# Second attention layer: value products in plain fp32 on two column halves, one exponent per slot, softmax sums added on GpSimd

## The chip, the core and the metric

One NeuronCore of a Trainium2 chip runs the whole program in one launch. The metric is the device time in microseconds (us), as the median of several runs. The engines are TensorE (PE; PEld is its weight load), VectorE (DVE), ScalarE (ACT), GpSimd (POOL) and SyncE (SP, which issues most DMAs). They run their own instruction streams and wait for each other on semaphores.

## What is computed

The program is two decoder layers on `x` (8 batch elements of 100 tokens, 256 wide) with a context `ctx` of 1444 keys of 64 numbers per batch element. The first layer is a causal attention with a mixture-of-experts feed-forward. The change touches only the attention of the second layer:

```python
q_big  = rope(einsum(x @ Wq.T, w_kc_q))          # per head, 192 wide
kv_r   = rope(ctx)                               # (1444, 64), shared by all 16 heads
q_r    = einsum(q_big, W_qr);  k_r = einsum(kv_r, W_kr)
attn   = softmax(einsum(q_r, k_r))               # (16 heads, 100, 1444)
ctx_c  = einsum(attn, kv_r)                      # (16 heads, 100, 64)
x      = x + (ctx_c @ w_kc_kv) @ Wo.T
```

It is followed by an 8-bit quantised gated feed-forward (`bit_linear`). Everything is float32 in and out.

## The kernel before, in words

The second layer runs batch element by batch element (`b` = 0 to 7). One batch element is 48 **slots** (`SLOTS = NG * KT`): four head groups of 4 heads x 100 queries (400 columns, `HT`), and for each of them 12 key tiles of 120 or 121 keys (`KT`). Each engine has one hand-written loop over `b` and slot `s`, and everything that is not a score or a value product is hung on a slot number by the constants at the head of the file.

In a slot PE makes the scores of one key tile (`scores`, L1025 to L1035): two fp32r matmuls, the high parts of q and k against both parts (128 rows) and then the low part of q with a row of negated maxima (65 rows). ACT takes the exponent twice from the same PSUM bank (L1421 into `pt`, plain fp32; L1422 into `ph`, fp32r, which is rounded). POOL subtracts the two (L619) so that `pl` holds the rounded rest. Three slots later (`LAG = 3`) PE adds the value product (`values`, L1037 to L1047): three fp32r matmuls, high weights with high and with low values and low weights with high values. The high value tile has a column of ones, so row 64 of the result is the softmax sum. There are three `pt` buffers and four of `ph` and `pl`.

After each group of 12 slots ACT copies the sum row and the context out of PSUM (`keep_context`), PE turns the sums into a column (`turn_sums`, L1057), DVE inverts them (L1668, 100x4), PE spreads the inverse over 64 partitions (`spread_sums`, L1066), and DVE multiplies (`divide`, L1677). This happens four times per batch element.

Beside this, in slots 0 to 12, the queries and keys of batch element `b + 1` are made: `q_big` (L972, L976) on PE, `rope` on DVE, `q_latent` (L990, 12 matmuls of 64 output columns by 100), `keep_q` on ACT, `low_q` on DVE; `turn_keys` (L1002) with `keep_keys` on ACT. `rotate_keys` on POOL makes the keys of `b + 2` (six pieces). In slots 14 to 40 thirteen **maximum tiles** bound the scores of `b + 1` (`max_tile`, L1017: three fp32r matmuls of 482 columns into three banks; `reduce_max`, L1654: three DVE reductions, which free the banks). The output projection (`attention_out`, L1075, slot 8) and the feed-forward of `b - 1` (`turn_xq`, `gate_and_up`, `turn_hq`, `ffn_down` on PE; `quantise_x`, `hidden`, `quantise_h` on DVE; `norm_x4` and `norm_h` on POOL; a Silu and a Square on ACT) are hung on slots 8 to 41. Batch element 7 has no next one to prepare, and batch element 0 has no feed-forward beside it.

On PE all of this is one in-order stream; a wait stops all that stands behind it. On POOL, `norm_x4` and `norm_h` stand in the same queue as the subtractions.

## Time and profile before

| what | us |
|---|---|
| median of 3 runs (1206.18 to 1210.96) | 1210.91 |
| the profiled execution: its own time | 1210.05 |
| its span, first to last instruction | 1208.0 |
| start of batch element 0's slots | 442.7 |
| one batch element in the middle (b = 3, 718.1 to 813.8) | 95.7 |
| slots of the last batch element | 1101.0 to 1172.6 |
| busy: PE, DVE, ACT, POOL | 1050.0, 530.6, 565.0, 579.8 |
| mean granted TensorE clock | 0.914 of 2.4 GHz |

Busy times are of the whole span, which has stages with different limits, so the stages have to be read one by one. A plain fp32 matmul leaves two MATMUL records in the trace, an fp32r matmul one. The length of a matmul's record includes the time for its results to arrive; what a matmul costs in a stream is the distance between two starts.

### The profile page before, as it was taken

The page shows a single profiled execution, that of the slowest core. Times are in us where ns is not written, and L with a number is a line of the kernel's source. Part 1 is how long each engine was busy: PE and PEld are TensorE (multiplying, and loading weights), DVE is VectorE, ACT ScalarE, POOL GpSimd, SP SyncE. Part 2 cuts the span into 40 slices and gives each one's busy share as a digit, 9 for nine tenths or more (in the row PEclk, how much of TensorE's full clock was granted, in tenths as well). Part 3 has the DMA queues.
Part 4 walks back from the last instruction along what each step waited for, and adds up shares of the span by engine and source line. Part 5 has one row for each costly group of instructions (what it writes and reads, how often), then busy time and mean ns, then how long its engine had stood idle before and what let it go on. Part 6 is the DMA issues. An engine that isn't in the chain of part 4 may idle for free.

```text
span 1208.0 us, 18195 instructions
## 1 busy us (share of the span) xinstructions
PE 1050.0 (87%) x6674; PEld 841.2 (70%) x6674; DVE 530.6 (44%) x1063; ACT 565.0 (47%) x1205; POOL 579.8 (48%) x787
## 2 busy tenths in 40 slices
PE   6986776788882879999999999999999999999883
PEld 3665665457872748888788678778778778877572
DVE  3234552333202663544743653563473473472423
ACT  2322222101212215765765664764665675577761
POOL 2002230244004007767676676676677575376760
PEclk9767887889996969999999999999999999999986
DMA  9015001516761000000000000000000000000000
GB/s 242 4 48 162 1 1 50 197 39 220 269 222 46 1 13 1 1 14 1 1 17 1 1 17 2 1 17 1 1 1 17 1 1 5 1 1 5 1 4 3
DMA packets 37827, 49.25 MB, mean 41 GB/s; under 512 B 9798, under 2 KB 31352, under 8 KB 37484
## 3 DMA queue, kind: packets, MB, share of 16 engines
q1 hardware_dynamic: 36716, 46.46, 12.4%
q0 software_dynamic: 1024, 1.64, 0.4%
q8 instruction: 53, 0.87, 0.3%
q14 instruction: 34, 0.28, 0.1%
HBM read 42.73 MB, written 5.31 MB: 40 GB/s over the span
## 4 chain that ended last, share of the span: by engine, by line
PE 61%; DVE 14%; issue 9%; POOL 6%; ACT 6%; DMA 2%; SPq 0%; POOLq 0%; DVEq 0%; ACTq 0%
PE ps L1033 8%; PE ps L990 5%; PE ps L972 5%; DVE nm L1654 5%; PE ps L913 4%; PE ps L1017 4%; PE ps L1047 4%; PE ps L1044 4%; PE ps L1045 4%; POOL pl L619 3%; PE ps L976 3%; PE ps L1075 2%; PE ps L1066 2%; PE ps L926 2%; PE ps L734 2%
## 5 line engine op out<-in xcount | busy, mean ns | idle before, releaser
L619 POOL TENSOR_TENSOR pl<-pt,ph 120x400 fp32r<-120x400 f32 (+1 forms) x384 | 407.5, 1081 | 282.4 <-ACT ph L1422 238.6
L1421 ACT ACTIVATE pt<-ps 120x400 f32<-120x400 f32 (+1 forms) x384 | 193.8, 505 | 154.3 <-PE ps L1033 150.7
L1654 DVE TENSOR_REDUCE nm<-ps 128x1 f32<-128x482 f32 (+1 forms) x312 | 184.1, 650 | 39.7 <-PE ps L1017 39.1
L1422 ACT ACTIVATE ph<-ps 120x400 fp32r<-120x400 f32 (+1 forms) x384 | 192.0, 500 | 0.0
L1033 PE MATMUL ps<-qh,khl 128*120 128x400 f32 (+1 forms) x384 | 149.7, 390 | 8.8 <-ACT ph L1422 5.6
L1033 PE MATMUL ps<-ql,kh 65*120 65x400 f32 (+1 forms) x384 | 135.1, 352 | 0.0
L1047 PE MATMUL ps<-pl,kv 120*65 120x400 f32 (+1 forms) x384 | 134.2, 349 | 0.4 <-POOL pl L619 0.2
L1044 PE MATMUL ps<-ph,kv 120*65 120x400 f32 (+1 forms) x384 | 134.2, 350 | 0.0
L1045 PE MATMUL ps<-ph,kv 120*64 120x400 f32 (+1 forms) x384 | 133.5, 348 | 0.0
L1017 PE MATMUL ps<-khl,qh 128*128 128x482 f32 (+1 forms) x312 | 101.5, 419 | 6.1 <-DVE ql L1646 1.7
L1633 DVE TENSOR_TENSOR xyz<-ps,ropeq 128x400 f32<-128x400 f32 x64 | 33.8, 570 | 157.3 <-PE ps L976 157.3
L1033 PEld LDWEIGHTS ps<-qh,khl 128*120 128x120 f32 (+1 forms) x384 | 72.0, 188 | 31.1 <-ACT ph L1422 9.9
L1354 ACT ACTIVATE qh<-ps 64x400 fp32r<-64x400 f32 x64 | 31.8, 497 | 116.7 <-PE ps L990 116.3
L1017 PEld LDWEIGHTS ps<-khl,qh 128*128 128x128 f32 (+1 forms) x312 | 57.9, 193 | 32.0 <-DVE nm L1654 14.5
L568 POOL TENSOR_TENSOR sm<-sm,mx 100x1600 f32<-100x1600 f32 x8 | 22.9, 2862 | 112.9 <-DVE mx L1501 112.9
L1033 PEld LDWEIGHTS ps<-ql,kh 65*120 65x120 f32 (+1 forms) x384 | 72.4, 189 | 4.2
L990 PE MATMUL ps<-xyz,amat 128*64 128x100 f32 x768 | 72.7, 251 | 0.2 <-DVE ql L1646 0.2
L990 PEld LDWEIGHTS ps<-xyz,amat 128*64 128x64 f32 x768 | 66.5, 137 | 5.5 <-issue 3.4
L972 PE MATMUL ps<-x3T,wqb 128*128 128x100 f32 x512 | 67.3, 288 | 2.8 <-DVE xyz L1637 2.2
L972 PEld LDWEIGHTS ps<-x3T,wqb 128*128 128x128 f32 x512 | 65.7, 204 | 5.1 <-DVE xyz L1637 2.5
L1047 PEld LDWEIGHTS ps<-pl,kv 120*65 120x65 f32 (+1 forms) x384 | 52.7, 137 | 20.5 <-POOL pl L619 2.4
L1045 PEld LDWEIGHTS ps<-ph,kv 120*64 120x64 f32 (+1 forms) x384 | 53.3, 139 | 18.2
(250 smaller groups left out, 1592.8 us busy)
## 6 DMA issues: line engine op xcount, KB each, us to landing
egu<-_L_ffn_gate_up_proj_dram SPq DMA_DIRECT2D x14, 1024.0 KB, 5.6
edn<-in_L_ffn_down_proj_dram SPq DMA_DIRECT2D x14, 512.0 KB, 6.4
craw<-in_ctx_dram SPq DMA_DIRECT2D x8, 360.0 KB
wo_n<-in_L_xattn_Wo_dram SPq DMA_DIRECT2D x1, 2048.0 KB, 11.7
wq_n<-in_L_xattn_Wq_dram SPq DMA_DIRECT2D x1, 2048.0 KB, 9.7
xs_scratch<-zero SPq DMA_DIRECT2D x1, 1792.0 KB, 12.9
xs<-xs_scratch SPq DMA_DIRECT2D x14, 128.0 KB, 5.5
ys_scratch<-ysb SPq DMA_DIRECT2D x14, 128.0 KB, 5.8
```

The lines of the kernel that those rows point to most:

```text
L619: nc.gpsimd.tensor_tensor(pl[k % PS_BUF][r, :], pt[k % PT_BUF][r, :], ph[k % PS_BUF][r, :].bitcast(F32), ALU.subtract).then_inc(pl_ready, 1)
L913: last = mm(ps[:, 2 * (t % 2) + a, TR * m:TR * m + TR], egu[t % EBUF][:, c, FI * a + 128 * m:FI * a + 128 * m + 128], xsT[t % 2][:, c, :], ...
L972: mm(ps[:, 4, S * i:S * i + S], wqb[:, c, h, 0:128], x3T[:, c, :], start=c == 0, stop=c == DC - 1)
L990: last = mm(ps[0:CD, 6, S * i:S * i + S], amat[:, h, j, :], xyz[k % 2][:, j, i, :], start=j == 0, stop=j == 2)
L1017: mm(ps[0:w, max_bank(b, i) + n, 0:MN], qh[b % 2][:, 128 * i:128 * i + w], khl[b % 2][:, MSTART[n]:MSTART[n] + MN], start=True, stop=True) ...
L1033: last = mm(ps[0:key_rows(t), k % 2, 0:HT], lhs[:, keys], rhs[:, HT * c:HT * c + HT], start=first, stop=not first)
L1044: mm(bank[0:CD + 1, :], w[r, t, CD:2 * CD + 1], hi[r, :], start=t == 0, stop=False)
L1045: mm(bank[0:CD, :], w[r, t, 0:CD], hi[r, :], start=False, stop=False)
L1047: mm(bank[0:CD + 1, :], w[r, t, CD:2 * CD + 1], lo[r, :], start=False, stop=t == KT - 1).then_inc(pv_done, 1)
L1421: nc.scalar.activation(pt[k % PT_BUF][0:rows, :], ps[0:rows, k % 2, 0:HT], ACT.Exp)
L1422: nc.scalar.activation(ph[k % PS_BUF][0:rows, :], ps[0:rows, k % 2, 0:HT], ACT.Exp).then_inc(ph_ready, 1)
L1654: nc.vector.tensor_reduce(nm3[0:w, i, n:n + 1], ps[0:w, max_bank(b, i) + n, 0:MN], AX.X, ALU.max)\
```

## The change

- Scores: a slot is still one key tile by one head group, but two slots in a row now take the same key tile for groups c and c + 2. A **pair** of slots is one step of the value product; there are 24 pairs and two rounds of 12 (`LANE` = 24 slots) per batch element.
- ACT takes one exponent per slot, into one half of `pt` (5 buffers of 120 x 2 x 400, plain fp32).
- The value product of a pair is two plain fp32 matmuls of 64 output columns, group c into partitions 0 to 63 and group c + 2 into partitions 64 to 127 of one bank. The value tile is the plain 64 columns.
- The softmax sums: POOL adds the `pt` tiles of a round (`add_weights`, 11 additions of 120x800 per round, each waiting for the one before), PE sums over the partitions with a matrix of ones (`sum_weights`, two matmuls), DVE inverts 128x400 and multiplies 128x400 (`divide`). The turn, the spread and the copy of the sum row are gone.
- `rotate_keys` loses a copy and a subtraction; the low part of the keys is made by DVE from PSUM (`low_keys`, three of 64x480 per batch element).
- `q_latent` writes two heads on the two column halves in turn; `keep_q` and `low_q` become four and two instructions of half the width.
- `max_tile` uses only the high parts, 64 rows each: tiles 0 and 2 on rows 0 to 63, tile 1 on rows 64 to 127. Its first matmul waits for the second reduction of the tile before, not the first.
- Some slots move by one or more; the divide stands at slot 7 of a round.

```diff
-KEEP_AT, TURN_AT, SPREAD_AT = 3, 4, 5
+KEEP_AT, SUM_AT, DIVIDE_AT = 3, 5, 7
-KEY_SLOT = (8, 9, 11)
+KEY_SLOT = (9, 10, 12)
-OUT_SLOT = 8
+OUT_SLOT = 9
-X4_SLOT, H_NORM_SLOT = 10, 24
+X4_SLOT, H_NORM_SLOT = 11, 24
-PT_BUF, PS_BUF = 3, 4
+PT_BUF = 5
@@ rotate_keys (POOL)
-            step(nc.gpsimd.tensor_tensor(kraw[r, :, :], kcos[r, :, :], ksin[r, :, :], ALU.add))
-            step(nc.gpsimd.tensor_copy(k[r, t, CD:2 * CD], kraw[r, :, :]))
-            nc.gpsimd.tensor_tensor(k[r, t, 0:CD], kraw[r, :, :], k[r, t, CD:2 * CD].bitcast(F32), ALU.subtract)\
-                .then_inc(kv_ready, 1)
+            nc.gpsimd.tensor_tensor(k[r, t, :], kcos[r, :, :], ksin[r, :, :], ALU.add).then_inc(kv_ready, 1)
@@ new (POOL), called in every odd slot
+        def add_weights(pool, j):
+            q, t = j // KT, j % KT
+            pool.wait_ge(p_ready, 2 * j + 2)
+            if t == 0:
+                return
+            r, total = slice(0, key_rows(t)), acc[q % 2]
+            if t == 1 and q >= 2:
+                pool.wait_ge(sums_done, q - 1)
+            if t > 1:
+                pool.wait_ge(p_added, (KT - 1) * q + t - 1)
+            before = pt[(j - 1) % PT_BUF] if t == 1 else total
+            nc.gpsimd.tensor_tensor(total[r, :, :], before[r, :, :], pt[j % PT_BUF][r, :, :], ALU.add).then_inc(p_added, 1)
@@ POOL's loop
-                    nc.gpsimd.tensor_tensor(pl[k % PS_BUF][r, :], pt[k % PT_BUF][r, :], ph[k % PS_BUF][r, :].bitcast(F32),
-                                            ALU.subtract).then_inc(pl_ready, 1)
+                    if s % 2:
+                        add_weights(pool, PSLOTS * b + s // 2)
@@ q_latent (PE)
-                for i in range(HG):
-                    h = HG * g + i
+                for i in range(0, HG, 2):
                     for j in range(3):
-                        last = mm(ps[0:CD, 6, S * i:S * i + S], amat[:, h, j, :],
-                                  xyz[k % 2][:, j, i, :], start=j == 0, stop=j == 2)
+                        for a in range(2):
+                            last = mm(ps[CD * a:CD * a + CD, 6, S * (i // 2):S * (i // 2) + S], amat[:, HG * g + i + a, j, :],
+                                      xyz[k % 2][:, j, i + a, :], start=j == 0, stop=j == 2)
@@ max_tile (PE)
-                    if before >= 0:
+                    if before >= 0 and n:
                         pe.wait_ge(m_reduced, 3 * before + n + 1)
-                    mm(ps[0:w, max_bank(b, i) + n, 0:MN], qh[b % 2][:, 128 * i:128 * i + w],
-                              khl[b % 2][:, MSTART[n]:MSTART[n] + MN], start=True, stop=True).then_inc(m_done, 1)
+                    elif before >= 0:
+                        pe.wait_ge(m_reduced, 3 * before + 2)
+                    r, keys = slice(CD * (n % 2), CD * (n % 2) + CD), khl[b % 2] if n % 2 else kh1[b % 2]
+                    mm(ps[0:w, max_bank(b, i) + n, 0:MN], qh[b % 2][r, 128 * i:128 * i + w],
+                              keys[r, MSTART[n]:MSTART[n] + MN], start=True, stop=True).then_inc(m_done, 1)
@@ values and the sums (PE)
-                mm(bank[0:CD + 1, :], w[r, t, CD:2 * CD + 1], hi[r, :], start=t == 0, stop=False)
-                mm(bank[0:CD, :], w[r, t, 0:CD], hi[r, :], start=False, stop=False)
-                pe.wait_ge(pl_ready, k + 1)
-                mm(bank[0:CD + 1, :], w[r, t, CD:2 * CD + 1], lo[r, :], start=False, stop=t == KT - 1).then_inc(pv_done, 1)
+                for a in range(2):
+                    last = mm(ps[CD * a:CD * a + CD, 2 + q % 2, 0:HT], kv[b % KV_BUF][r, t, :], pt[j % PT_BUF][r, a, :],
+                              start=t == 0, stop=t == KT - 1)
+                last.then_inc(pv_done, 1)
+            def sum_weights(q):
+                pe.wait_ge(p_added, (KT - 1) * (q + 1))
+                if q:
+                    pe.wait_ge(c_ready, q)
+                for a in range(2):
+                    last = mm(ps[CD * a:CD * a + CD, 7, 0:HT], ones[0:KP, :], acc[q % 2][:, a, :], start=True, stop=True)
+                last.then_inc(sums_done, 1)
@@ ACT's loop
-                    nc.scalar.activation(pt[k % PT_BUF][0:rows, :], ps[0:rows, k % 2, 0:HT], ACT.Exp)
-                    nc.scalar.activation(ph[k % PS_BUF][0:rows, :], ps[0:rows, k % 2, 0:HT], ACT.Exp).then_inc(ph_ready, 1)
+                    if j >= PT_BUF and k % 2 == 0:
+                        act.wait_ge(pv_done, j - PT_BUF + 1)
+                        act.wait_ge(p_added, added(j - PT_BUF))
+                    nc.scalar.activation(pt[j % PT_BUF][0:rows, k % 2, :], ps[0:rows, k % 2, 0:HT], ACT.Exp).then_inc(p_ready, 1)
@@ divide (DVE)
-                tt(ct[p, cols], ctu[p, cols], ps[p, 7, 0:HT], ALU.mult).then_inc(c_ready, 1)
+                step(nc.vector.reciprocal(inv[:, :], ps[:, 7, 0:HT]))
+                tt(ct[:, cols], ctu[:, cols], inv[:, :], ALU.mult).then_inc(c_ready, 1)
```

## Rows read from the trace of the kernel before

**Rows 1.** The page: span and busy times of the engines.

```profile
span 1208.0 us, 18195 instructions
PE 1050.0 (87%) x6674; PEld 841.2 (70%) x6674; DVE 530.6 (44%) x1063; ACT 565.0 (47%) x1205; POOL 579.8 (48%) x787
```

**Rows 2.** Busy time by stretch (b = 3 in four parts, b = 0, b = 7).

```profile
core 0: us, PE busy (x) PEld busy (x) DVE busy (x) ACT busy (x) POOL busy (x), PEclk, DMA share, GB/s
718.10:757.60 39.50, 39.23 (x305) 34.43 (x303) 13.31 (x33) 19.62 (x43) 27.03 (x50) 1.00 0.02 5
757.60:776.70 19.10, 17.29 (x86) 12.74 (x86) 9.68 (x20) 14.66 (x29) 10.73 (x13) 0.91 0.00 0
776.70:808.10 31.40, 30.64 (x174) 23.50 (x173) 25.39 (x47) 20.42 (x45) 23.72 (x22) 1.00 0.01 2
808.10:813.80 5.70, 5.70 (x35) 4.76 (x33) 0.81 (x2) 4.98 (x12) 4.07 (x5) 1.00 0.21 51
...
442.70:528.00 85.30, 84.10 (x525) 70.61 (x526) 38.00 (x75) 52.49 (x118) 60.61 (x83) 0.95 0.03 10
...
1101.00:1172.60 71.60, 63.97 (x348) 49.92 (x347) 22.96 (x33) 52.23 (x113) 49.93 (x50) 0.93 0.01 2
```

**Rows 3.** Timeline of PE in ordinary slots: start us, length us, engine, line.

```profile
620.39 0.34 PE L1033 MATMUL ps<-qh,khl 128*120 128x400 f32 x1
620.57 0.34 PE L1033 MATMUL ps<-ql,kh 65*120 65x400 f32 x1
...
621.30 0.34 PE L1033 MATMUL ps<-qh,khl 128*120 128x400 f32 x1
```

**Rows 4.** Timeline of PE around a query product and a spread of sums.

```profile
633.50 2.27 PE L990 MATMUL ps<-xyz,amat 128*64 128x100 f32 x24
...
635.70 0.45 PE L1033 MATMUL ps<-qh,khl 128*120 128x400 f32 x1
635.99 0.34 PE L1033 MATMUL ps<-ql,kh 65*120 65x400 f32 x1
...
636.53 0.34 PE L1047 MATMUL ps<-pl,kv 121*65 121x400 f32 x1
636.81 0.90 PE L1066 MATMUL ps<-ident,inv 100*64 100x100 f32 x8
637.64 0.45 PE L1033 MATMUL ps<-qh,khl 128*120 128x400 f32 x1
637.92 0.34 PE L1033 MATMUL ps<-ql,kh 65*120 65x400 f32 x1
```

**Rows 5.** Timeline of PE in the set-up: two fp32 products on column halves.

```profile
79.98 0.65 PE L739 MATMUL ps<-woT,kckv_n 128*64 128x256 f32 x4
80.56 0.66 PE L722 MATMUL ps<-ident,wo_n 128*128 128x128 f32 x4
```

**Rows 6.** Groups of POOL instructions by shape: busy us, mean ns.

```profile
L619 POOL TENSOR_TENSOR pl<-pt,ph 120x400 fp32r<-120x400 f32 x256 | 270.6, 1073 | 189.1 <-ACT ph L1422 148.0 <-issue 28.2 <-PE ps L1047 7.4
L568 POOL TENSOR_TENSOR sm<-sm,mx 100x1600 f32<-100x1600 f32 x8 | 22.9, 2862 | 112.9 <-DVE mx L1501 112.9
L503 POOL TENSOR_TENSOR kraw<-kcos,ksin 120x128 f32<-120x128 f32 x32 | 14.6, 457 | 2.5
```

**Rows 7.** Groups of DVE reciprocals by shape.

```profile
L1668 DVE RECIPROCAL inv<-ps 100x4 f32<-100x4 f32 x32 | 5.7, 180 | 49.4 <-PE ps L1057 49.3
L1530 DVE RECIPROCAL rec<-ps 100x16 f32<-100x16 f32 x8 | 2.0, 252 | 2.9 <-PE ps L844 2.9
```

**Rows 8.** Groups on DVE in 776.7 to 808.1.

```profile
L1654 DVE TENSOR_REDUCE nm<-ps 128x1 f32<-128x482 f32 (+1 forms) x33 | 19.5, 650 | 3.2 <-PE ps L1017 3.1
L1716 DVE SCALAR_TENSOR_TENSOR h<-h,rstdh,lnw_b 100x1024 f32<-100x1024 f32 x1 | 1.3, 1286 | 0.0
L1677 DVE TENSOR_TENSOR ct<-ctu,ps 64x400 f32<-64x400 f32 x2 | 1.1, 563 | 0.2 <-PE ps L1066 0.2
```

**Rows 9.** Timeline of POOL and DVE in the last batch element.

```profile
1118.97 7.09 POOL L619 TENSOR_TENSOR pl<-pt,ph 120x400 fp32r<-120x400 f32 x7
1119.04 5.15 DVE L1692 TENSOR_SCALAR xn<-x_sb,mv,rstd 100x256 f32<-100x256 f32 x1 [2.77 <-POOL rstd L529]
...
1142.71 6.03 DVE L1716 SCALAR_TENSOR_TENSOR h<-h,rstdh,lnw_b 100x1024 f32<-100x1024 f32 x1 [3.41 <-POOL rstdh L529]
```

**Rows 10.** The chain that ended last: the last division.

```profile
1177.77 0.58 DVE ct L1677
```

168 lines of the change are left out of this document (72 added, 96 removed).

## The prediction

> **What bounds the kernel now.** I read the page first [rows 1]: PE is busy 87% of the span, no other engine over half. Then the busy times by stretch [rows 2], because the second layer (442.7 to the end) is where the change lies. In the middle of the layer one batch element takes 95.7 us, and I cut it in four by what runs beside the slots. Slots 0 to 12 (39.5 us, with the queries and keys of the next element) have PE busy 39.2: PE sets the pace. Slots 13 to 22 (19.1 us) have 1.8 us of PE idle and wait on the feed-forward's chain through DVE, POOL and ACT. Slots 23 to 41 (31.4 us) have PE busy 30.6 and DVE 25.4, which is close behind. Slots 42 to 47 (5.7 us) are PE alone. The last element takes 71.6 us with PE idle for 7.6. Then the timeline for what a matmul costs: an ordinary slot is five fp32r matmuls from 620.39 to 621.30, so 0.91 us, or 0.182 each [rows 3].
>
> **What the change does to PE in a slot.** Removed: three value matmuls, 3 x 0.182 = 0.546 us per slot. Added: per pair two plain fp32 matmuls of 400 columns on the two column halves. The trace has the same thing in the set-up: L739 is two fp32 products of 256 columns on two column halves, four records, in 0.65 us, and the next group starts 0.58 us after it [rows 5]. A record of 256 columns at fp32 is 256 x 2 / 2.4 GHz = 0.213 us, so four in a row would start the next group after 0.85; two and two are 0.43, and 0.58 is that and 0.15 for the ends. So the halves run side by side. For 400 columns: 2 x 0.333 = 0.667 us per pair.
>
> **The ends are the catch.** Between an fp32r matmul of full width and a product of 64 columns the stream stops [rows 4]. L1047 starts at 636.53 and has 0.167 of columns, so it is through at 636.70; L1066 starts at 636.81: 0.11 us lost, and about 0.05 until its first weights are in. L1066's eight records start 0.083 to 0.086 apart and are through at 637.54; the next score matmul starts at 637.64, and the one behind it 0.28 later instead of 0.182, because its weights were not loaded ahead: 0.19 us lost. After L990 it is the same (635.70 to 635.99). I take 0.35 us for going there and back, so a value pair costs 0.667 + 0.35 = 1.02 us against 2 x 0.546 = 1.09 now. The plain slots gain almost nothing. (The Trainium skill, "TensorEngine Tiling (Array Packing)", Key Properties, states that changing the tiling mode drains the engine; this rule speaks against the change, the rows above agree with it, and without it the pair would be 0.67.)
>
> **Other PE terms, per batch element.**
> - The turn and the spread of sums go, four times. From L1047's end (636.70) to the next score matmul's real start (637.74) the spread is 1.0; the turn I take as the same. 4 x 2.0 = 8 us.
> - `sum_weights`, two times: one more value pair, 1.0 each, 2 us. It waits for POOL's last addition of the round; the cover is five slots of PE work (over 4 us, over 7 where `q_big` lies between), and POOL needs about 2 per addition, so it costs nothing unless POOL is more than two additions behind.
> - `q_latent`: 24 records 0.086 apart (2.27 with the end) [rows 4] become 12 pairs: 1.03 saved, four times, 4.1 us. It had the switch already.
> - `turn_keys` has 64 output columns now and gets the switch, 3 x 0.3 = 0.9 us.
> - `max_tile`: three matmuls of 482 columns are 3 x 0.2 = 0.60. With two of them side by side they are 0.40, and the switch adds 0.35: +0.15, thirteen times, +1.9 us. Bounds: 0.2 less each if there is no switch, +0.35 if the row halves don't overlap.
>
> **Stage by stage, b = 1 to 6.** Slots 0 to 12: -13 x 0.546 - 2.0 - 4.1 = -13.2; +6.5 x 1.02 + 1.0 + 0.9 = +8.5; so PE -4.7. `q_big` of the second group waits for DVE's rope of the first, which now has some 2 us of slots before it instead of 3.9 and needs about 2.7: +0.7. Stage: -4.0.
> Slots 13 to 41: PE -29 x 0.546 - 2 x 2.0 = -19.8; +14.5 x 1.02 + 1.0 + 1.9 = +17.7: -2.1. But here DVE is the next limit. It is busy 35.1 of the 50.5 us [rows 2], and the rest of its time is mostly waits in the feed-forward chain that stay. It loses two inversions and two multiplications of 0.56 and 0.18 [rows 7, 8], -1.5, and gains one `divide`: the reciprocal of 128x400. The rows give 180 ns at 4 elements and 252 at 16, so 6 ns each: 0.16 + 400 x 0.006 = 2.5 us, the upper bound; one like a multiplication of 400 (0.56) is the lower; I take 2.5, the only rows of the same operation. With the multiplication 3.1. So DVE gains 1.6 us. Further it is held by POOL (below), +2 to +4. I take -1.0 for the stage.
> Slots 42 to 47: PE -0.2; zero. Sum per element: -5. Six of them: -30.
> Element 0 has no feed-forward, so PE's sums hold: -4.7 - 2.1 - 0.2 = -7.
>
> **POOL.** An addition of 120x800 is in no row. 457 ns at 128 elements and 1073 at 400 [rows 6] are 2.26 ns an element, so 1.98 us; by the 100x1600 row (2862) it is 1.67. I take 2.0 and 0.08 for the wait on the one before. 22 per element are 46 us, the rotated keys 6 x 1.6 = 10, the norms 1: 57 of some 90 us. POOL is behind a pair in the plain slots (2.08 against PE's 4 x 0.182 + 1.02 = 1.75) and catches up elsewhere; five buffers carry that. ACT has half its exponents and is nowhere the limit; `low_keys` and the halves of `low_q` and `keep_q` add some 2.5 us to DVE in slots 0 to 12, where it is busy 13.3 of 39.5 [rows 2]; that cover would have to shrink by half before it shows.
>
> **The last element.** From 1101.0 to the last division, 1177.77 [rows 10], it is 77.4 us. POOL sets the pace now: 22 x 2.08 + norms + 3 us start + some 3 us of waits for the norms = 53, then the sum, the reciprocal and the multiplication (4.5), and stalls of the feed-forward that the buffers don't cover, 5: 63. That is -14; I give it 0 to -20, as PE's clock is less sure there (0.93 now). The start-up of element 0 (DVE-bound maxima) I leave at 0 to +2.
>
> **Sum:** -30 - 7 - 14 = -51, and +1 for the start, -50. Against the profiled execution's own time, 1210.05 (0.9 below the median of the three runs), 1160 us.
>
> **The rivals.**
> 1. *No drain, or a cheaper one.* If the weights for the value pair are pulled ahead of the scores, 0.35 x 24 = 8.4 us of PE per element go. In slots 0 to 12 and for element 0 they are time, in slots 13 to 41 DVE keeps most of it: about -4 per element and -8 for element 0, so -35: 1125. Against it: three transitions of the same two kinds in the rows, all with it. For it: DVE or POOL may set the pace so that the drains lie in waits.
> 2. *DVE held by POOL* (slower). In the last element DVE's L1692 takes 5.15 us while POOL runs seven subtractions back to back, and L1716 takes 6.03 where it takes 1.29 undisturbed [rows 8, 9]. POOL's additions are twice as long, and six DVE instructions per element read and write only SBUF in this way (three in `quantise_x`, three in `quantise_h`), and the new multiplication of `divide`. I have counted 2 to 4 us per element, because each addition waits for the one before and leaves a gap. If two of them per element are held for 5 to 6 us instead, that is +9 in slots 13 to 41, PE waits behind `turn_xq` and the maxima, and the sum turns: 1160 + 7 x 9 = 1223. It decides from 7 us per element. (The Trainium skill, "SBUF — State Buffer", describes the pair of ports that DVE and GpSimd share as an exclusive lock held for a whole instruction. By it each holding is one addition, up to 2 us, seven times 1 on average: the sum above plus about 3 per element, 1180; the 5.15 us row shows more than one instruction.)
> 3. *The halves don't overlap* (slower). Then a value pair is 1.33 + 0.35, 16 us more per element, and `q_latent` and the sums 5.5: 1160 + 8 x 21 = 1330. Rows 5 speak against it.
> 4. *The clock.* Slots 13 to 22 have a mean of 0.91 [rows 2], so 19.1 x 0.09 x 2 = 3.4 us of them at 1.2 GHz. If PE, with more short gaps, gets one more such stretch per element, each costs 1.7: 1174. It is within my range.
>
> **How the numbers follow.** Forecast (1140 to 1185, with rival 4) 0.60; rival 1 and cheaper terms (1095 to 1140) 0.21; between 1185 and 1204 0.05; no change 0.04; rival 2 0.08; rival 3 0.02. A measurement of this kernel tells 0.5%, 6 us, from no change. The likeliest value is 1160; eight in ten lie in 1105 to 1205. Faster by over 0.5%: 0.86, within: 0.04, slower: 0.10.
>
> **What would show it.** Right: two MATMUL records of the value pair starting within some 10 ns of each other, twice per pair; value pair and switch near 1.0 us between score matmuls; an element near 90 us; a reciprocal of 2.5 us; additions near 2.0; DVE busy over 37 us in slots 13 to 41. Wrong: score matmuls behind the values with their weights loaded ahead, an element under 85; DVE instructions of several us beside the additions; PE idle in slots 42 to 47 for POOL; a granted clock below 0.9 in the middle of the layer.

## The result and the profile after

The changed kernel takes 1285.97 us (median of 4 runs, 1282.71 to 1288.57) beside 1210.93 for the kernel before on the same chip (1206.18 to 1216.58): the ratio is 1.0616, with a 95% interval of 1.0564 to 1.0669. It is 6% slower; the forecast was 4% faster.

The page of the changed kernel, its span and busy times. Against [rows 1] there is less work of every kind but DVE's, and PE is busy for 18 us *longer*:

```profile
span 1281.0 us, 15373 instructions
PE 1068.0 (83%) x5842; PEld 655.6 (51%) x5842; DVE 598.5 (47%) x1087; ACT 397.6 (31%) x837; POOL 473.6 (37%) x480
```

832 fewer matmuls and more busy time are longer matmuls. A part of it is by design, since each of the two records of a plain fp32 matmul is longer than that of an fp32r one; the rest shows in the granted clock. Of both kernels the busy times from the first slot to the last of the layer: span, busy of PE, PEld, DVE, ACT and POOL, then the granted clock, DMA share and GB/s. First the kernel before:

```profile
442.70:1172.60 729.90, 703.25 (x4424) 572.43 (x4425) 355.78 (x719) 462.59 (x991) 490.92 (x612) 0.98 0.02 5
```

and the changed kernel:

```profile
444.50:1242.10 797.60, 727.49 (x3604) 391.32 (x3604) 416.96 (x736) 293.94 (x615) 390.45 (x333) 0.81 0.02 5
```

The granted clock of the whole layer falls from 0.98 to 0.81. The levels are 1.00 (2.4 GHz) and 0.50 (1.2 GHz), nothing between. Added up, the stretches at 0.50 from the layer's first slot to the end of the span are 55.3 us before and 338.1 after.

The same batch element as in [rows 2] (b = 3, slots 0 to 12, 13 to 22, 23 to 41, 42 to 47), then three windows within it and the last element's slots:

```profile
762.50:797.60 35.10, 32.90 (x279) 24.66 (x277) 17.57 (x38) 12.86 (x31) 19.12 (x27) 1.00 0.02 6
797.60:819.50 21.90, 19.21 (x63) 8.06 (x60) 10.98 (x20) 11.39 (x21) 10.36 (x11) 0.69 0.00 0
819.50:861.00 41.50, 36.77 (x130) 15.74 (x129) 28.84 (x45) 11.59 (x23) 18.50 (x11) 0.74 0.00 1
861.00:867.20 6.20, 6.20 (x28) 3.08 (x26) 0.81 (x2) 2.95 (x7) 3.57 (x2) 0.84 0.25 64
802.00:815.00 13.00, 13.00 (x34) 5.30 (x35) 7.94 (x15) 4.14 (x7) 6.55 (x4) 0.50 0.00 0
815.50:839.00 23.50, 19.74 (x83) 8.10 (x82) 19.60 (x29) 10.94 (x20) 11.84 (x7) 1.00 0.00 1
839.10:861.00 21.90, 20.66 (x62) 9.18 (x62) 10.64 (x19) 4.31 (x8) 7.50 (x4) 0.50 0.00 1
...
1181.20:1242.10 60.90, 55.65 (x240) 28.43 (x238) 24.81 (x29) 27.83 (x56) 43.06 (x25) 0.89 0.01 2
```

Slots 0 to 12 take 35.1 us where they took 39.5: the part in which the clock stays up is as forecast. Slots 13 to 41 take 63.4 where they took 50.5, and slots 42 to 47, which a stretch reaches into, 6.2 where they took 5.7. In each of the six middle elements the trace has at least two stretches at 1.2 GHz: one begins at slot 14 and lasts 13.7 us, the other begins at the maximum tile behind slot 34 and lasts 20.5 or 23.9 us, to slot 41, 42 or 43, where the maximum tiles end. The same element had 3.4 us in all in the kernel before.

Element 0, which has no feed-forward, is hit hardest. It takes 106.8 us where it took 85.3, with two stretches of 34.1 us each, one from slot 14 and one from slot 35 into the next element. They follow waits of 2.33 and 2.74 us:

```profile
444.50:551.30 106.80, 99.46 (x439) 51.59 (x440) 42.66 (x78) 33.21 (x73) 49.48 (x46) 0.69 0.03 8
```

What PE did before the second stretch, in the timeline of PE (start us, length us, engine, line; in brackets the idle time before it and who ended it):

```profile
834.03 0.44 PE L1042 MATMUL ps<-qh,khl 128*120 128x400 f32 x1
834.31 0.35 PE L1042 MATMUL ps<-ql,kh 65*120 65x400 f32 x1
834.59 0.89 PE L1053 MATMUL ps<-pt,kv 121*64 121x400 f32 x4
835.41 0.45 PE L1042 MATMUL ps<-qh,khl 128*120 128x400 f32 x1
835.70 0.34 PE L1042 MATMUL ps<-ql,kh 65*120 65x400 f32 x1
839.66 0.74 PE L1026 MATMUL ps<-kh,qh 64*128 64x482 f32 x1 [3.62 <-DVE nm L1650]
839.66 0.76 PE L1026 MATMUL ps<-khl,qh 64*128 64x482 f32 x1
```

The maximum tile (L1026, its first two matmuls side by side on the row halves) waited 3.62 us for the reductions that free its banks. The clock falls at 839.1, at the end of this wait, and the tile is the first work at the lower clock. DVE's timeline says why they were late:

```profile
829.20 3.66 DVE L1650 TENSOR_REDUCE nm<-ps 128x1 f32<-128x482 f32 x6
832.77 2.65 DVE L1673 RECIPROCAL inv<-ps 128x400 f32<-128x400 f32 x1
835.46 2.13 DVE L1674 TENSOR_TENSOR ct<-ctu,inv 128x400 f32<-128x400 f32 x1
837.51 0.74 DVE L1721 TENSOR_SCALAR h<-h,qsc 100x1024 f32<-100x1024 f32 x1
838.28 1.79 DVE L1650 TENSOR_REDUCE nm<-ps 128x1 f32<-128x482 f32 x3
```

From 832.77 to 838.28 the divide and one multiplication of the feed-forward stand in front of the reductions. The first stretch begins in the same way, at the element's first maximum tile, which waits for the last part of the next keys:

```profile
799.22 0.35 PE L1042 MATMUL ps<-ql,kh 65*120 65x400 f32 x1
801.89 0.77 PE L1026 MATMUL ps<-kh,qh 64*128 64x482 f32 x1 [2.32 <-DVE khl L1664]
```

The page's groups for the new operations (busy us, mean ns of one | idle before it) stand against [rows 6 and 7]:

```profile
L525 POOL TENSOR_TENSOR acc<-acc,pt 120x800 f32<-120x800 f32 (+1 forms) x160 | 302.3, 1890 | 338.3 <-ACT pt L1414 259.8
L1673 DVE RECIPROCAL inv<-ps 128x400 f32<-128x400 f32 x16 | 42.5, 2654 | 19.8 <-PE ps L1065 19.5
```

An addition takes 1.89 us (2.0 forecast), a reciprocal 2.65 (2.5 forecast), and POOL idles for 338 us before its additions, mostly for the exponents: it isn't behind PE here.

### The profile page after: what moved, and what is told of

The parts are those of the page before. It is cut to its first block, busy times and chain, and to the rows that moved or that the text cites. A ratio compares the mean times of both kernels' runs of the same rounds, so it can differ in the third digit from the quotient of the medians.

```text
span 1281.0 us, 15373 instructions
## 1 busy us (share of the span) xinstructions
PE 1068.0 (83%) x5842; PEld 655.6 (51%) x5842; DVE 598.5 (47%) x1087; ACT 397.6 (31%) x837; POOL 473.6 (37%) x480
## 4 chain that ended last, share of the span: by engine, by line
PE 66%; DVE 16%; issue 7%; ACT 5%; POOL 3%; DMA 2%; SPq 0%; POOLq 0%; DVEq 0%; ACTq 0%
PE ps L1042 13%; PE ps L1053 12%; PE ps L1026 6%; PE ps L978 5%; DVE nm L1650 4%; PE ps L919 4%; PE ps L996 3%; PE ps L1073 3%; PE ps L982 2%; DVE inv L1673 2%; PE ps L932 2%; PE ps L740 2%; ACT qh L1350 1%; DVE xyz L1629 1%; PE ps L1119 1%
## 5 line engine op out<-in xcount | busy, mean ns | idle before, releaser
L525 POOL TENSOR_TENSOR acc<-acc,pt 120x800 f32<-120x800 f32 (+1 forms) x160 | 302.3, 1890 | 338.3 <-ACT pt L1414 259.8
L1053 PE MATMUL ps<-pt,kv 120*64 120x400 f32 (+1 forms) x768 | 214.2, 644 | 0.0
L1042 PE MATMUL ps<-qh,khl 128*120 128x400 f32 (+1 forms) x384 | 192.7, 502 | 4.7 <-DMA ql<-nmr 3.1
L1026 PE MATMUL ps<-kh,qh 64*128 64x482 f32 (+1 forms) x208 | 103.2, 572 | 53.7 <-DVE nm L1650 33.9
L1026 PEld LDWEIGHTS ps<-kh,qh 64*128 64x128 f32 (+1 forms) x208 | 42.8, 238 | 111.8 <-issue 73.2
L1053 PEld LDWEIGHTS ps<-pt,kv 120*64 120x64 f32 (+1 forms) x768 | 43.9, 157 | 65.5 <-issue 55.4
L1350 ACT ACTIVATE qh<-ps 64x200 fp32r<-64x200 f32 x128 | 42.5, 332 | 82.7 <-PE ps L996 81.3
L919 PE MATMUL ps<-xsT,egu 128*128 128x128 f32 x448 | 54.9, 282 | 12.5 <-issue 11.5
L1026 PE MATMUL ps<-khl,qh 64*128 64x482 f32 (+1 forms) x104 | 64.5, 621 | 0.0
L919 PEld LDWEIGHTS ps<-xsT,egu 128*128 128x128 f32 x448 | 52.9, 197 | 16.8 <-issue 15.2
```

Source lines behind the costliest of these rows:

```text
L525: nc.gpsimd.tensor_tensor(total[r, :, :], before[r, :, :], pt[j % PT_BUF][r, :, :], ALU.add).then_inc(p_added, 1)
L919: last = mm(ps[:, 2 * (t % 2) + a, TR * m:TR * m + TR], egu[t % EBUF][:, c, FI * a + 128 * m:FI * a + 128 * m + 128], xsT[t % 2][:, c, :], ...
L1026: mm(ps[0:w, max_bank(b, i) + n, 0:MN], qh[b % 2][r, 128 * i:128 * i + w], keys[r, MSTART[n]:MSTART[n] + MN], start=True, stop=True).then_ ...
L1042: last = mm(ps[0:key_rows(t), k % 2, 0:HT], lhs[:, keys], rhs[:, HT * c:HT * c + HT], start=first, stop=not first)
L1053: last = mm(ps[CD * a:CD * a + CD, 2 + q % 2, 0:HT], kv[b % KV_BUF][r, t, :], pt[j % PT_BUF][r, a, :], start=t == 0, stop=t == KT - 1)
L1350: last = nc.scalar.activation(own[:, :, a, :], ps[CD * a:CD * a + CD, 6, 0:2 * S].rearrange("p (i q) -> p i q", q=S), ACT.Copy)
```

## The experiments

Two theories were open. **Rows** (A in the expectations): the 64-row maximum matmuls keep the clock at 1.2 GHz once it is there. **Waits** (C): what brings it there is PE's long waits at slots 14 and 34, which the change's divide and its order on ACT and DVE made. Their rival (B) is that the 64-column value products keep it down; other rivals are told where a run tests them. In every run with half rows the first matmul of a tile also waits for the second reduction of the tile before, as in the change, and in every run with full rows for the first. No run takes the two apart, so "the rows" below means the tile as changed. One table first, since the expectations refer to one another. "At 1.2 GHz" is the sum of the 0.50 stretches from the layer's first slot to the end, "layer" the time between these two, "b = 3" that element; the ratio is to the kernel before on the same chip, whose median is 1210.9 for runs 1 to 4, 1211.0 for 5 to 8 and 1211.8 for 9 to 11. The last three columns are of one profiled execution each, which can lie beside the median (10 us below it in run 3).

| run | median us | ratio (95%) | at 1.2 GHz | layer | b = 3 |
|---|---|---|---|---|---|
| before | 1210.9 | | 55.3 | 765.3 | 95.7 |
| changed | 1286.0 | 1.062 (1.056 to 1.067) | 338.1 | 836.5 | 104.7 |
| 1: full rows | 1218.1 | 1.006 (1.003 to 1.009) | 192.0 | 772.3 | 97.4 |
| 2: divide in parts | 1242.2 | 1.029 (1.022 to 1.035) | 229.3 | 789.1 | 98.2 |
| 3: both | 1199.3 | 0.991 (0.988 to 0.994) | 133.6 | 748.0 | 95.1 |
| 4: before, half rows | 1215.9 | 1.004 (1.002 to 1.006) | 36.3 | 766.7 | 95.6 |
| 5: both, queries first | 1165.9 | 0.964 (0.960 to 0.969) | 86.8 | 718.3 | 91.4 |
| 6: filler | 1277.6 | 1.056 (1.051 to 1.061) | 238.2 | 825.3 | 105.8 |
| 7: 5, values by two | 1196.9 | 0.988 (0.984 to 0.992) | 90.2 | 745.5 | 95.6 |
| 8: before, DVE block | 1258.8 | 1.039 (1.035 to 1.043) | 96.1 | 812.9 | 104.2 |
| 9: 5, half rows | 1196.2 | 0.990 (0.984 to 0.995) | 153.7 | 740.8 | 91.8 |
| 10: 8, half rows | 1288.6 | 1.062 (1.058 to 1.066) | 158.8 | 841.5 | 107.3 |
| 11: low rows only | 1311.9 | 1.084 (1.080 to 1.087) | 351.9 | 853.7 | 106.2 |

**1. Full rows.** The changed kernel with the maximum tiles of the kernel before: three matmuls over 128 rows, one after the other, with their waits.

```diff
-                    if before >= 0 and n:
+                    if before >= 0:
                         pe.wait_ge(m_reduced, 3 * before + n + 1)
-                    elif before >= 0:
-                        pe.wait_ge(m_reduced, 3 * before + 2)
-                    r, keys = slice(CD * (n % 2), CD * (n % 2) + CD), khl[b % 2] if n % 2 else kh1[b % 2]
-                    mm(ps[0:w, max_bank(b, i) + n, 0:MN], qh[b % 2][r, 128 * i:128 * i + w],
-                              keys[r, MSTART[n]:MSTART[n] + MN], start=True, stop=True).then_inc(m_done, 1)
+                    mm(ps[0:w, max_bank(b, i) + n, 0:MN], qh[b % 2][:, 128 * i:128 * i + w],
+                              khl[b % 2][:, MSTART[n]:MSTART[n] + MN], start=True, stop=True).then_inc(m_done, 1)
```

> The changed kernel with one part undone: the maximum tiles on all 128 rows again, as before (their first matmul waits for the first reduction again). In the changed kernel one batch element has two stretches of TensorE at 1.2 GHz, together some 35 of 104.7 us, and both lie among the maximum tiles, while the last element, which has none, has only short ones. Theory A (the 64-row matmuls keep the clock from coming back): mean clock from 0.805 to 0.88 or more, an element at 90 to 95 us, 1286 becomes 1180 to 1215. Theory B (the 64-column fp32 value products do it): clock and time within 1% of the changed kernel, the switch of 0.15 us per tile aside. Theory C (only the long waits of TensorE count, and here they are the same): no difference beyond 1%.

Measured: 68 us less from this edit, the direction of Theory A, though the median (1218), the clock (0.857) and the element (97.4) each lie just outside what it said. Its three matmuls are the longer ones, and it is faster all the same. The wait behind slot 34 is still there, 3.04 us, and still starts a stretch; but in its windows (first the stretch, then the rest up to slot 42) the clock is back after 6.8 us, not after 23.9:

```profile
803.40:810.20 6.80, 5.60 (x14) 3.18 (x15) 4.66 (x9) 1.01 (x2) 1.88 (x1) 0.50 0.00 0
810.20:820.80 10.60, 9.02 (x49) 4.79 (x48) 7.07 (x13) 3.25 (x6) 4.95 (x3) 1.00 0.00 1
```

In the six middle elements these second stretches are 6.8 or 10.2 us long, in the changed kernel 20.5 or 23.9. The first stretches are 10.2 instead of 13.7; four elements have 3.4 us more at slot 12, where the changed kernel has it in one. Element 0 falls from 106.8 to 86.8 us, so 20 of the 68 us are its own. Between these two kernels the rows decide how long the clock stays down, not whether it falls. PE's different wait for the reductions is hardly the reason: within a long stretch with half rows it waits little (1.24 of 21.90 us above, 0.29 of 23.70 in run 6).

**2. Divide in parts.** The changed kernel; the divide of the first round is made as four reciprocals and multiplications of 128x100 in slots 31, 33, 35 and 38 (the new `divide_part` is left out here). The other round's divide, at slot 7, stays in one piece.

```diff
-                    if (b or s >= LANE) and s % LANE == DIVIDE_AT:
-                        divide(PAIRS * b + s // LANE - 1)
+                    if b and s == DIVIDE_AT:
+                        divide(PAIRS * b - 1)
+                    if s in PART_SLOT:
+                        divide_part(PAIRS * b, PART_SLOT.index(s))
```

> The changed kernel with the division of the first round (slot 31) cut into four pieces of 100 columns at slots 31, 33, 35 and 38. The second stretch at 1.2 GHz begins where TensorE waits 3.6 us for VectorE behind a reciprocal of 2.65 and a multiplication of 2.13 us. Theory C (a wait starts the stretch): the second stretch, 20 to 24 us at 1.2 GHz per element, gets shorter or goes; 1286 becomes 1200 to 1240. Theories A and B (it is what the array is given that keeps the clock low, and any wait will start it): it begins a little later at some other wait; within 2% of the changed kernel.

Measured: 44 us less than the changed kernel (its executions range from 1232.9 to 1251.4, so 35 to 53). Each theory has a part of it. The wait of 3.62 us is gone, and the second stretch is shorter: none in b = 1, 3.4 us in b = 2, 10.2 in the other four. But it is still there, as A and B had it: in these four it now starts at slot 39, behind a wait of 0.93 us, and runs to slot 43. The wait in b = 3:

```profile
821.66 0.51 PE L1113 MATMUL ps<-ident_bf,hq 100*128 100x100 bf16 x8 [0.93 <-DVE nm L1651]
```

**3. Both.** Edits 1 and 2 together.

> Both edits together. If A holds alone this equals the run with full rows (within 1%); if A and C both hold it is the fastest, 1150 to 1185, near the 1160 that the sum at full clock gave; if B holds neither helps and it stays at 1270 to 1290.

Measured: 87 us less for both, where 68 and 44 would sum to 112; at 1199 it misses the 1150 to 1185 that was expected if A and C both hold. The second stretch is gone from b = 2, 5 and 6 and is 3.4 or 6.8 us in b = 1, 3 and 4, behind the same wait of 0.93 us at slot 38 or 39 that 10.2 us follow in run 2: with the short waits there is less for the rows to prolong. Most of what is left in the middle elements is the first stretch, at slots 12 to 20. Version 3 is already faster than the kernel before, by 0.9%.

**4. The kernel before with half rows.** Only `max_tile` as in the change; values, exponents and divides of before.

> The kernel before with one part of the change: its maximum tiles on 64 rows, tiles 0 and 2 on rows 0 to 63 and tile 1 on rows 64 to 127 (high parts only). By the prediction's term it is 13 x 0.15 us per element slower, 7 elements, so +14 us, at an unchanged clock. Theory A: the stretch of 3.4 us at 1.2 GHz at slots 17 and 18 gets longer, clock below 0.90, +25 us or more. Theory B: clock as before (0.914), +5 to +20 us.

Measured: 1.004, as Theory B said, and 36.3 us at 1.2 GHz where the kernel before has 55.3: no stretch begins in elements 0 to 6, where the kernel before has one of 3.4 us in each of b = 2 to 6. The window from 700 to 800 us, longer than an element, has a granted clock of 1.00:

```profile
700.00:800.00 100.00, 97.02 (x615) 73.70 (x614) 54.28 (x109) 62.37 (x134) 69.49 (x90) 1.00 0.02 6
```

So 64-row matmuls alone bring nothing down, and alone they bring no gain either. This is the run that would have cleared the maximum tiles if the edits had been tried one at a time.

**5. Queries first.** Version 3 with ACT's copy of the next queries (`keep_q`) ahead of its copy of the next keys where both fall on one slot. In the changed kernel it stood behind them, DVE's `low_q` waited for it, and the last `low_keys`, behind that on DVE, came late for the first maximum tile.

```diff
+                        if s in LAT_SLOT:
+                            keep_q(b + 1, LAT_SLOT.index(s))
                         if s in KEY_SLOT:
                             keep_keys(b + 1, KEY_SLOT.index(s))
-                        if s in LAT_SLOT:
-                            keep_q(b + 1, LAT_SLOT.index(s))
```

> The kernel with full rows and the division in parts, and in slots 10 and 12 ScalarE copies the queries before the keys (TensorE writes them in that order). In that kernel the first maximum tile waits 1.5 us and the query product of slot 12 waits 1.7 us, behind copies of keys that came first; the first stretch at 1.2 GHz begins there. Theory C (long waits of TensorE start the stretches): the stretch at slots 13 to 20 (10 us in element 3) gets shorter or goes, 1199 becomes 1165 to 1185. Rival (the feed-forward's own waits at slots 17 to 22 start it anyway): within 0.7% of 1199.

Measured: 1165.9 us, the fastest version of the study, 3.6% below the kernel before, as Theory C said (1165 to 1185). It has the change's 64-column value products in every pair, so Theory B falls: they don't hold the clock down by themselves. The four parts of b = 3, to be read against [rows 2]:

```profile
704.40:737.80 33.40, 32.89 (x278) 24.63 (x277) 17.57 (x38) 13.10 (x32) 17.90 (x27) 1.00 0.02 6
737.80:757.80 20.00, 16.15 (x62) 8.07 (x60) 10.63 (x20) 11.12 (x21) 11.64 (x11) 0.83 0.00 0
757.80:790.40 32.60, 30.58 (x128) 15.17 (x127) 28.41 (x51) 11.48 (x23) 17.95 (x11) 0.95 0.00 1
790.40:795.80 5.40, 5.40 (x29) 2.63 (x27) 0.81 (x2) 2.83 (x7) 4.16 (x3) 1.00 0.25 69
```

The wait of the first maximum tile is 1.02 us (2.32 in the changed kernel), and 3.4 to 10.2 us per middle element stay at 1.2 GHz, most of it at slots 17 and 18, behind a wait of 2.4 us for the feed-forward's input (4.0 in b = 6). In its plain slots the period of a pair can be read, with every term of the forecast at full clock:

```profile
792.28 0.44 PE L1040 MATMUL ps<-qh,khl 128*120 128x400 f32 x1
792.56 0.35 PE L1040 MATMUL ps<-ql,kh 65*120 65x400 f32 x1
792.74 0.35 PE L1040 MATMUL ps<-qh,khl 128*120 128x400 f32 x1
792.93 0.34 PE L1040 MATMUL ps<-ql,kh 65*120 65x400 f32 x1
793.20 0.89 PE L1051 MATMUL ps<-pt,kv 120*64 120x400 f32 x4
794.02 0.44 PE L1040 MATMUL ps<-qh,khl 128*120 128x400 f32 x1
```

The pair takes 1.74 us (794.02 - 792.28; forecast 1.75), the values 0.82 and 0.09 + 0.10 us more go at their two ends. That is 1.01 us, 0.34 over the 0.667 of columns; the forecast had 1.02 and 0.35.

**6. Filler.** Is it the rows of the maximum tiles, or would any full-width work bring the clock back? The changed kernel, with one more 128-row score matmul per slot in slots 13 to 41; its product is overwritten.

```diff
+                if b < B - 1 and 13 <= k % SLOTS <= 41:
+                    mm(ps[0:key_rows(t), k % 2, 0:HT], khl[b % 2][:, keys], qh[b % 2][:, HT * c:HT * c + HT],
+                       start=True, stop=True)
```

> The changed kernel with work added: in slots 13 to 41 of elements 0 to 6 each score begins with one more full-width fp32r matmul, 128x120 by 400, that the real first one overwrites. It costs 29 x 0.18 = 5.2 us of TensorE per element at full clock. Theory A in its wide form (the clock stays at 1.2 GHz because the 64-row and 64-column matmuls and the stops around them are too little for it, and any full-width work brings it back): 37 us at 1.2 GHz per element become less than 15, and with more work the kernel is faster, 1286 becomes 1240 to 1270. Rival (waits alone set the clock): time at 1.2 GHz per element stays at 34 us or more, and the kernel gets slower, 1300 to 1330.

Measured: neither outcome in full. With 36 us of work added the kernel is 8 us faster, and 100 us less are at 1.2 GHz. Most of that is in element 0, whose two stretches of 34.1 us are gone (3.4 us are left besides those at its start, and it takes 86 us instead of 106.8), and in b = 1, which has no long second stretch. The first stretches are shorter too (6.8 to 13.7 us). But in b = 2 to 6 the second ones are 23.9 us long and end with the maximum tiles (the window of one):

```profile
824.90:848.60 23.70, 23.41 (x71) 11.88 (x70) 9.99 (x19) 5.02 (x10) 7.50 (x4) 0.50 0.00 1
```

PE is busy for 23.41 of its 23.70 us and the clock stays down. Only 7 of the 71 matmuls are the added ones, though, since a slot is long there. So this little full-width work beside the 64-row tiles doesn't bring the clock back, while taking the 64-row tiles out (run 1) does; what more of it would do isn't shown, and in element 0 some of it went with the end of the stretches.

**7. Values by two.** Version 5 with the values of two pairs together, every fourth slot, so that half of the drains go. `KEEP_AT` moves from 3 to 4, because the values of a round end later.

```diff
-                    if k >= LAG and k % 2 == LAG % 2:
+                    if k % 4 == LAG:
+                        if k > LAG:
+                            values((k - LAG) // 2 - 1)
                         values((k - LAG) // 2)
```

> The kernel of the run with the queries first, and the value products of two pairs behind each other in every fourth slot, so that TensorE goes to the 64-column form and back 12 times per element instead of 24. By the prediction's term this saves 12 x 0.35 = 4.2 us of TensorE per element at full clock: 20 to 33 us less than the run with the queries first, if TensorE sets the pace. Rival (VectorE sets the pace in slots 13 to 41): only slots 0 to 12 and 42 to 47 gain, 8 to 14 us less. If the switch is no cost of its own: no change.

Measured: 31 us slower than version 5, which none of the three expected. Two pairs of b = 3:

```profile
806.67 1.56 PE L1051 MATMUL ps<-pt,kv 120*64 120x400 f32 x8
808.17 0.44 PE L1040 MATMUL ps<-qh,khl 128*120 128x400 f32 x1
...
809.39 0.44 PE L1040 MATMUL ps<-qh,khl 128*120 128x400 f32 x1 [0.23 <-ACT pt L1414]
...
810.33 1.56 PE L1051 MATMUL ps<-pt,kv 120*64 120x400 f32 x8
```

The values of two pairs take 1.50 us (808.17 - 806.67), where two of 0.82 and the ends between them would be 1.83: one drain is saved. But there are only two banks of scores, four scores in a row outrun ACT, and PE waits. Two pairs take 3.66 us (810.33 - 806.67) against 3.48 in version 5, at about the same time at 1.2 GHz (90.2 and 86.8). Over 96 such groups that is 17 of the 31 us. Of the rest a part is the first maximum tile, which waits 2.04 us here and 1.02 in version 5. Whether more score banks would give the gain of the prediction's rival 1 wasn't tried.

**8. A block on DVE in the kernel before.** Four reciprocals of 128x200 at slot 31, on a tile that nothing else reads: the change's divide block by itself, with the old tiles and values (the lines that make the tile are left out).

```diff
+                    if s == 31:
+                        for i in range(4):
+                            step(nc.vector.reciprocal(junk[:, :], junk[:, :]))
```

> The kernel before with VectorE blocked at slot 31 by four reciprocals of 128x200 on a tile of their own (some 5.5 us per element), as the changed kernel's division blocks it. VectorE has about 6 us to spare in slots 23 to 41. Theory A with C (a wait starts a stretch at 1.2 GHz, but full-width fp32r work ends it at once): each element gets one stretch of 3.4 us or none, +10 to +35 us in all. Rival (the wait alone explains the long stretch of the changed kernel): 14 us or more at 1.2 GHz per element after slot 31, +60 us or more.

Measured: ratio 1.039, 48 us more, between the two expectations. A maximum tile waits 4.57 us, and in the six middle elements the clock falls behind slot 34 for 3.4 or 6.8 us. Slots 23 to 41 of b = 3 go from 31.4 us to 39.0:

```profile
823.70 0.74 PE L1018 MATMUL ps<-khl,qh 128*128 128x482 f32 x1 [4.57 <-DVE nm L1655]
```

```profile
801.70:840.70 39.00, 33.53 (x175) 25.40 (x173) 31.05 (x51) 20.39 (x45) 22.60 (x22) 0.91 0.01 1
```

5.7 us of DVE work cost 7.6 us. PE is idle for 5.5 us of the stage instead of 0.8, which is 4.7, and busy 2.9 longer, which is the clock's share (6.8 us at 1.2 GHz cost at most 3.4). Busy time of 25.4 in 31.4 us had looked like 6 us to spare; for a block in one piece there is little.

**9. Version 5 with half rows.** The short waits stay, the change's tiles come back.

> e5 with the change's own maximum tiles (64 rows, two side by side) put back; the earlier queries and the divide in four parts stay. Theory that the long PE waits alone start and keep the stretches at 1.2 GHz: they stay as in e5, about 7 to 10 us at 1.2 GHz per middle element, elements 89 to 92, median 1160 to 1172. Theory that the 64-row maxima keep the clock from coming back once it has fallen: each of the two falls that e5 still has becomes a stretch of 10 us or more, 20 us or more at 1.2 GHz per middle element, elements 96 to 100, median 1200 to 1235. The sum of the single effects read so far gives a point between: e2 (1242) less what the earlier queries brought beside e3 (33) is 1209.

Measured: 1196.2 us, 30 above version 5 and between the two theories. Two of the six middle elements (b = 2, 5) have a single stretch of 6.8 us at slot 18, as version 5 has in such places; in b = 1 and 4 a stretch of 20.5 us starts behind slot 35 and runs to slot 43; in b = 3 and 6 the first one is 13.7. The second stretch of b = 1 begins at 608.0, and PE's only idle time of more than 0.35 us ahead of it since 591.4 is this one:

```profile
606.22 0.46 PE L1027 MATMUL ps<-kh,qh 64*128 64x482 f32 x1 [0.75 <-DVE nm L1651]
```

So with half rows a long wait isn't needed: 0.75 us went ahead of 20.5 us at 1.2 GHz. In version 5 with full rows the wait at this point is shorter (0.36 us) and no stretch follows in b = 1. The effects aren't a sum. Shorter waits and order take 90 us from the changed kernel with half rows and 52 with full rows (1218.1 to 1165.9). Full rows take 68 us with both long waits in place, 43 with the divide in parts (runs 2 and 3) and 30 with both waits shortened.

**10. Run 8 with half rows.** The values of the kernel before, the block, and the change's tiles.

> The kernel before, with the block of reciprocals on DVE at slot 31 (as in e8, where the PE wait of 4.6 us is followed by 6.8 us at 1.2 GHz) and with the change's 64-row maximum tiles. The value products and all else are those of the kernel before. Theory that the 64-row tiles alone keep the clock down after a long wait: the stretch behind the wait runs until the maximum tiles end, at about slot 43, so 17 us or more at 1.2 GHz per middle element beside 6.8 in e8, slots 23 to 41 at 43 to 47 us, elements 105 to 110, median 1290 to 1340. Theory that the change's value products (64 output columns in fp32) are needed for it too: 6.8 to 10 us at 1.2 GHz per element as in e8, elements 101 to 104, median 1255 to 1270.

Measured: 1288.6 us, 30 above run 8, and neither expectation holds. The stretches behind slot 34 are 6.8, 6.8, 13.7, 13.7, 27.3 and 13.7 us (b = 1 to 6; in run 8 6.8, 3.4, 6.8, 3.4, 6.8, 6.8). The longest, over nearly all of its length, with the old value products running:

```profile
1038.40:1065.10 26.70, 23.89 (x82) 15.51 (x83) 13.57 (x24) 8.06 (x17) 7.25 (x7) 0.50 0.00 1
```

So the changed tiles alone prolong what a wait started, by 2.4 times in sum (82 us against 34), without anything else of the change. In the changed kernel all six run to the end of the tiles (137 us). Whether the rest is the new value products or where the wait falls among the tiles stays open.

**11. Low rows only.** The changed kernel with all three matmuls of a tile on rows 0 to 63, one after the other.

```diff
-                    r, keys = slice(CD * (n % 2), CD * (n % 2) + CD), khl[b % 2] if n % 2 else kh1[b % 2]
+                    r, keys = slice(0, CD), kh1[b % 2]
```

> The changed kernel with all three maximum matmuls of a tile on rows 0 to 63, so that none runs beside another; rows per matmul stay 64. At full clock a tile costs 0.2 us more, 13 tiles in 7 elements: +18 us if nothing else changes. Theory that it is the 64 rows of a matmul that keep the clock down: the time at 1.2 GHz stays at 300 us or more, stretches in the middle elements end with the maximum tiles, median 1285 to 1330. Theory that it is two matmuls side by side on the row halves (and the change of the array's form at each of them): the clock comes back early as with 128 rows, 190 to 240 us at 1.2 GHz, median 1215 to 1250.

Measured: 1311.9 us, 351.9 us at 1.2 GHz, all six second stretches 23.9 us, as the theory of the 64 rows said. That two matmuls run side by side on the row halves is not what keeps the clock down. What is left of the difference to run 1 is the 64 rows of each matmul and the wait for the second reduction, of which the rows are the likelier, as said at run 1. Of the 26 us over the changed kernel the serial tiles at full clock would be 18 (0.2 x 13 x 7), and those in the stretches cost more.

**The price of the clock.** Six versions share the change's values, sums and exponents and differ in tiles, parts and order (5, 3, 9, 1, 2 and the changed kernel). Their layers against their time at 1.2 GHz: 718.3 at 86.8, 748.0 at 133.6, 740.8 at 153.7, 772.3 at 192.0, 789.1 at 229.3, 836.5 at 338.1. From the first to the last that is (836.5 - 718.3) / (338.1 - 86.8) = 0.47 us per us at 1.2 GHz, PE's loss of one half but for what it waits. The waits themselves and the other tiles are in this too, so it isn't the clock alone; between runs 8 and 10, which have the same block and nearly the same waits, it is 28.6 / 62.7 = 0.46. (The Trainium skill, "TensorE: Matmul & The Clock Gate", HAM oscillation, describes a kernel that falls to 1.2 GHz at each repeated wait and counts half of the time there as lost; the 0.47 agrees with the half. Its waits are of 3 to 5 us; here the clock also falls behind shorter ones, down to 0.63 us, and the measurement decides.)

## Why the prediction was wrong

**The step that failed is the clock, rival 4.** It allowed "one more such stretch per element" of 3.4 us, 1.7 us each, and so 1174 as its worst. Measured are 34 to 46 us per middle element at 1.2 GHz where at most 3.4 were before, 66 in element 0 where 8.7 were, and 283 us more in the layer. At 0.47 that is 133 us, and the profiled execution is 123 us above the forecast (1282.7 against 1160). Of these some 87 are in the six middle elements (105.0 us each on average, forecast near 90.5) and 28 in element 0 (106.8, forecast 78.3). The forecast named the right sign to look for, a clock below 0.9 in the middle of the layer, and priced it with the one stretch length that the trace of before happened to have. Two things were missing: where the stretches begin (behind a wait of PE at a place that could be named), and that their length isn't fixed (3.4 to 37.5 us among those that begin in elements 0 to 6 of these runs).

**The block on DVE was sized and not placed.** The reciprocal was taken as 2.5 us and is 2.65 (the line through rows of 4 and 16 elements was called an upper bound; that it comes so near at 400 is partly luck); "DVE gains 1.6 us" over slots 13 to 41 and "-1.0 for the stage" treated it as a sum. But it stands in one piece, with its multiplication, in front of the reductions that free PE's banks, and PE waits 3.62 us for it once per element. Run 8 shows that the kernel before couldn't hide such a block either (a PE wait of 4.57 us). In version 5, with the parts spread, slots 13 to 41 of b = 3 take 52.6 us (20.0 + 32.6) against 50.5 before: 2.1 more instead of 1.0 less, of which at most 3.4 is the clock (10.2 us at 1.2 GHz there, 3.4 before).

**A miscount.** The old kernel's turn, inversion, spread and division fall on three places in slots 13 to 41 (slots 16, 28 and 40 and the ones behind them), and the stage's sum takes off two. With three, PE's part is -4.1 and not -2.1, DVE loses 2.2 us and not 1.5, and element 0 comes to -9 and not -7. The layer's forecast was held by DVE there, so this changes it by about 2 us in element 0 and perhaps 4 in the six others.

**The maximum tiles** were costed at +0.15 us each, with bounds of -0.2 and +0.35, so 14 us for seven elements. Run 4, the kernel before with them alone, is 5 us slower by the medians and 1.4 in its layer, with 19 us less at 1.2 GHz, which are worth some 9 us at 0.47. So the term has the right sign and size, within what one profile tells. The real cost was in the stretches.

**The order of keys and queries on ACT** was in the diff as "some slots move by one or more"; I read DVE's added work in slots 0 to 12 as covered, and it is (4.3 us more, 2.5 forecast). But the last `low_keys` feeds the first maximum tile at slot 14, and there it is late by 2.32 us. What the cover hides from the stage's end it doesn't hide from the one instruction that needs its result.

**What held.** Slots 0 to 12: -4.4 us (-4.0 forecast), in version 5 -6.1. Slots 42 to 47 in version 5: 5.4 us (5.5 with "-0.2"). Pair: 1.74 us (1.75). Element 0 in version 5: 76.6 against 85.3, -8.7 (-7, or -9 counted right). The value pair's halves run side by side: their records in the changed kernel start at 823.349 and 823.356, and 823.736 and 823.743, 7 ns apart, so rival 3 falls. The drains are there (0.34 us per value pair), so rival 1 falls as the change stands. The last element from its first slot to the last division is 68.4 us (1181.2 to 1249.6) against 77.3 (1101.0 to 1178.3), -8.9 where -14 was forecast, within its 0 to -20. POOL is busy 43.1 of its first 60.9 us and not the pace that was forecast. Version 5, which keeps the change's values, sums and exponents and has 86.8 us at 1.2 GHz against 55.3 before, takes 1165.9 us, near the 1160. It isn't the kernel that was forecast, since its tiles, its divide and its order are others, and a part of the nearness is luck: slots 0 to 12 gain 2 us more than forecast and slots 13 to 41 lose 3 us more. The six middle elements together come to -28.7 us (-30 forecast).

**Rival 2, DVE held by POOL.** It takes place, in the size of one addition. The multiplication of the divide takes 0.57 us alone and 2.13 at 835.46, beside an addition that runs from 835.28:

```profile
835.28 1.88 POOL L525 TENSOR_TENSOR acc<-acc,pt 120x800 f32<-120x800 f32 x1 [0.68 <-ACT pt L1414]
```

Lengths of 5.15 and 6.03 us as in [rows 9] don't come back: but for the reciprocals, the longest DVE instruction in the last element is 2.38. The likely reason is that the additions wait for one another and leave a gap, where the subtractions ran back to back; no run tests it. (The Trainium skill, "SBUF — State Buffer", SBUF: two separate sides, has the shared ports locked for one whole instruction; 2.13 us is the end of the addition and the multiplication's own 0.57 to within 0.3 us, which agrees; the 5.15 us before is more than one instruction.) It isn't the cause of the loss, though 1.6 us of the 3.62 us wait are its part.

## What to carry to other kernels

Price a change by where PE waits first, not by busy sums: name the longest single block that a new operation puts in front of what frees PE's banks, and spread it (cutting one divide in four gave 44 us with half rows and 19 with full rows; copying the queries before the keys gave 46 and 33). In this kernel a maximum tile on half of the rows saved nothing at full clock (run 4) and kept TensorE at 1.2 GHz for longer after a wait, so try small products full where PE waits (68 us here with long waits, 30 with short ones). And when the granted clock is lower than before, count its stretches, find the wait in front of each and the kind of matmul in it, and treat their length as a result, not as a constant.
